# Local attention scores over all 128 rows on zero-spread keys, zero-padded values, agents' rows by broadcast load, and a new step order

## What is computed

```python
x = LN(x + agent_tok * agent_v[:, None, :])          # agent_v: one row of 256 per batch
x = LN(x + cross_attention(x, ctx, masks))           # ctx has 361 rows, one head
x = LN(x + attention over the top 50 tokens, 16 heads)
# local attention: 16 heads of 16 columns, keys within 64 positions
q, k, v = x @ Wq.T + bq, x @ Wk.T + bk, x @ Wv.T + bv
scores = einsum('bhtd,bhtwd->bhtw', q, kb) / sqrt(16);  scores = where(valid, scores, -inf)
x = LN(x + merge_heads(softmax(scores) @ vb) @ Wo.T + bo)
x = LN(x + cross_attention(x, ctx))
x = LN(x + quantize(rms_norm(x)) @ w_int8.T + bias)
```

## Time and profile before

| | |
|---|---|
| runs (3) | 1148.42, 1149.96, 1151.2 us, median 1149.96 us |
| the profiled execution | 1141.62 us, span 1139.5 us |
| granted PE clock, mean over the span | 0.861 of full speed |
| busy: PE, DVE, ACT, POOL | 85%, 62%, 48%, 28% of the span |

### The profile page before, as it was taken

How to read it: one execution, slowest core, us unless ns; L and a number is a source line. 1 busy time by engine, 2 the same in 40 slices (tenths; PEclk the granted TensorE clock), 3 DMA queues, 4 the chain that set the end, 5 groups by cost and what they waited for, 6 DMA issues and landing times.

```text
span 1139.5 us, 19498 instructions
## 1 busy us (share of the span) xinstructions
PE 963.4 (85%) x6958; PEld 706.0 (62%) x6958; DVE 705.2 (62%) x2131; ACT 542.9 (48%) x2440; POOL 315.8 (28%) x460
## 2 busy tenths in 40 slices
PE   6887988989787999886798799899899889998774
PEld 4665776656565766664476586466557666665552
DVE  4226675457787765535777755365848875556664
ACT  3112446667334257654434436556534345675431
POOL 0045211133542220403442320033344330122231
PEclk9857999879898899887889897688679798899676
DMA  7904100002221000010213000002201200000000
GB/s 206 279 22 134 36 2 1 1 21 81 83 89 70 15 1 2 22 54 28 77 40 122 16 1 2 1 22 75 76 28 55 70 15 1 1 2 1 8 8 15
DMA packets 21429, 50.78 MB, mean 45 GB/s; under 512 B 3376, under 2 KB 9236, under 8 KB 21332
## 3 DMA queue, kind: packets, MB, share of 16 engines
q1 hardware_dynamic: 21332, 49.53, 13.3%
HBM read 46.25 MB, written 3.28 MB: 43 GB/s over the span
## 4 chain that ended last, share of the span: by engine, by line
PE 52%; DVE 23%; ACT 17%; issue 3%; POOL 2%; DMA 1%; SPq 1%; DVEq 0%; POOLq 0%
PE psum L419 8%; PE psum L458 8%; ACT work L779 8%; PE psum L424 6%; ACT work L738 5%; PE psum L590 5%; PE psum L444 4%; DVE bn L896 4%; PE psum L604 3%; DVE x L903 2%; PE psum L596 2%; PE psum L610 2%; DVE res L944 1%; DMA ctxT<-in_x 1%; PE psum L414 1%
## 5 line engine op out<-in xcount | busy, mean ns | idle before, releaser
L779 ACT ACTIVATE work<-psum,mx 100x100 f32<-100x100 f32 x512 | 169.9, 381 | 63.3 <-DVE mx L1052 63.1
L779 ACT ACTIVATION_READ_ACCUMULATOR work<-psum,mx 100x1 f32 x512 | 124.6, 245 | 0.0
L1138 POOL TENSOR_SCALAR ve<-mv 100x2 f32<-100x2 f32 x96 | 22.4, 233 | 335.3 <-DVE mv L898 335.1
L458 PE MATMUL psum<-eT,ctx 128*128 128x100 f32 x768 | 102.9, 291 | 3.6 <-DVE eT L932 3.5
L458 PEld LDWEIGHTS psum<-eT,ctx 128*128 128x128 f32 x768 | 99.5, 207 | 6.5 <-DVE eT L932 5.1
L604 PE MATMUL psum<-ident,work 100*100 100x100 f32 x512 | 75.7, 285 | 30.8 <-ACT work L779 30.3
L444 PE MATMUL psum<-ctxT,qT 128*100 128x361 f32 x256 | 91.2, 502 | 5.1 <-ACT qT L669 2.9
L669 ACT ACTIVATE eT<-psum 100x400 f32<-100x400 f32 (+3 forms) x128 | 66.3, 532 | 45.6 <-PE psum L451 21.8
L604 PEld LDWEIGHTS psum<-ident,work 100*100 100x100 f32 x512 | 57.1, 148 | 47.9 <-ACT work L779 43.4
L590 PE MATMUL psum<-kT,qT 32*100 32x200 f32 x512 | 84.5, 410 | 2.7 <-DVE aT L1067 2.4
L1052 DVE TENSOR_REDUCE mx<-psum 100x4 f32<-100x400 f32 x128 | 66.9, 565 | 32.0 <-PE psum L596 31.4
(11 more groups left out here) (234 smaller groups left out, 2184.4 us busy)
## 6 DMA issues: line engine op xcount, KB each, us to landing
ctx<-in_ctx SPq DMA_DIRECT2D x16, 768.0 KB, 6.4
ctxT<-in_ctxT SPq DMA_DIRECT2D x16, 722.0 KB, 4.3
cell<-in_cell SPq DMA_DIRECT2D x16, 282.0 KB
seq<-in_seq SPq DMA_DIRECT2D x16, 282.0 KB
x<-in_x SPq DMA_DIRECT2D x16, 200.0 KB
out<-xplus SPq DMA_DIRECT2D x16, 200.0 KB
work<-in_x SPq DMA_DIRECT2D x4, 400.0 KB
ctx<-in_x SPq DMA_DIRECT2D x2, 400.0 KB
```

Of the source, the lines that this page charges most:

```text
L458: last = e.matmul(bk[b][:, c * S:(c + 1) * S], s.ctx[:, b, j, c * P:(c + 1) * P], s.pT[:, b, j, :], start=j == 0, stop=j == S2C - 1)
L779: last = e.activation(s.e[:, h, :], bk[g][0:S, q * S:(q + 1) * S], ACT.Exp, bias=s.mx[0:S, h:h + 1], accum_out=s.den[0:S, h:h + 1])
```

## The change

- Scores: both key halves leave PSUM with their bias only, into `s.kall`. For each unit POOL writes `s.keys` (128 rows by 8 times 100 columns), the keys multiplied with the constant mask `heads`, so that the columns of head h are zero outside of its 16 rows. Two matmuls over all 128 rows, 400 columns each, give the scores of eight heads, and one mask matmul follows each. The next unit's keys can be written as soon as the scores that read the tile are done.
- Values: `s.v` holds each head's 16 columns padded to 32 with zeros, set once by memset. Two heads then add up in one group of 32 PSUM rows, in 8 matmuls of 32 by 100 in place of 4 of 32 by 200, and nothing has to be picked out. The reciprocals are transposed ahead of them and leave PSUM through ACT meanwhile. DVE line 1064 is gone. One of the two value copies goes to DVE.
- Agents' rows: written once to a DRAM tensor and loaded for each job by a broadcast DMA into the end of `s.eT`; the matmuls of line 474 are gone, and DVE reads the row from SBUF.
- Small tiles of the agents' part share space with others; the memsets to zero of the values are waited for in the pick stage of the first turn and not ahead of it.
- `ORDER` has new strings for all engines.

```diff
-    "local": "xT q k0 k1 v0 v1 " + " ".join(f"hs{i} s{i} tra{i} trb{i} av{i}" for i in range(NB * NC)) + " out0 out1",
+    "local": "xT q k v0 v1 " + " ".join(f"s{i} tra{i} trb{i} R{i} av{i}" for i in range(NB * NC)) + " out0 out1",
...
-                pe, act, dve, pool = s.at("mix")
-                for b in range(NB):
-                    if t:
-                        e.wait_ge(*s.vector["quant"](f"r{b}", t - 1))
-                    n = NB * s.pair(t) + b
-                    e.matmul(bk[b][0:S, 0:D], ident[0:B, n:n + 1].to_broadcast([B, S]), agent_v[:, :],
-                             start=True, stop=True).then_inc(*pe.up(f"agv{b}"))
...
-                    for wave in range(2):
-                        if wave:
-
-                            e.wait_ge(*pe(f"hs{i}", t))
-                        for g in range(2):
-                            r = 32 * (2 * wave + g)
-                            last = e.matmul(bk[g][0:S, wave * T:(wave + 1) * T], s.qT[r:r + 32, c, b * S:(b + 1) * S],
-                                            s.kT[r:r + 32, :, c, b * S:(b + 1) * S], start=wave == 0, stop=False,
-                                            skip_group_check=True)
...
+                    e.wait_ge(*pool(f"bd{i}", t))
+                    for g in range(2):
+                        e.matmul(bk[g][0:S, 0:4 * S], s.qT[:, c, b * S:(b + 1) * S], s.keys[:, 4 * g:4 * g + 4, :],
+                                 start=True, stop=False, skip_group_check=True)
+                        last = e.matmul(edges(bk[g]), band_w[:, :],
+                                        band_x[:, :].rearrange("p (m k) -> p m k", m=2).unsqueeze(1).to_broadcast(
+                                            [NM, 4, 2, NEDGE]), start=False, stop=True, skip_group_check=True)
...
-                    for r in range(ROWS):
-                        e.matmul(bk[0][32 * r:32 * r + 32, 0:T], s.v[0:S, b, c * P + 32 * r:c * P + 32 * r + 32],
-                                 s.eT[0:S, r * T:(r + 1) * T], start=True, stop=True)
-                    e.wait_ge(*pool(f"re{i}", t))
-                    e.transpose(bk[1][:, 0:S], s.rspread[0:S, 0:P], ident[0:S, 0:S]).then_inc(*pe.up(f"av{i}"))
+                    e.wait_ge(*dve(f"eT{i}", t))
+                    e.wait_ge(*pool(f"re{i}", t))
+                    e.transpose(bk[1][:, 0:S], s.rspread, ident[0:S, 0:S]).then_inc(*pe.up(f"R{i}"))
                     e.wait_ge(*act(f"eT{i}", t))
+                    for j in range(2):
+                        for r in range(ROWS):
+                            h = 2 * r + j
+                            last = e.matmul(bk[0][32 * r:32 * r + 32, 0:S], s.v[0:S, b, c * HQ + h, :],
+                                            s.eT[0:S, h * S:(h + 1) * S], start=j == 0, stop=j == 1, skip_group_check=True)
...
-                    e.wait_ge(*act(f"u{i}", t))
-                    e.scalar_tensor_tensor(s.xT[:, 1, 0:S], bk[0][:, S:2 * S], own[:, 1:2], s.xT[:, 0, 0:S], ALU.mult,
-                                           ALU.add).then_inc(*dve.up(f"u{i}"))
...
             for s in streams:
-                last = e.memset(s.v_pick[:, :, :, :], 0.0)
+                e.memset(s.v_pick[:, :, :, :], 0.0)
+                last = e.memset(s.v[:, :, :, :], 0.0)
...
+            def blocks(t, i):
+
+                b, c = divmod(i, NC)
+                if i == 0:
+                    e.wait_ge(*s.vector["local"]("k1", t))
+                else:
+                    e.wait_ge(*s.tensor["local"](f"s{i - 1}", t))
+                e.tensor_tensor(s.keys[:, :, :], s.kall[:, c, b * S:(b + 1) * S].unsqueeze(1).to_broadcast([P, HQ, S]),
+                                heads[:, :].unsqueeze(2).to_broadcast([P, HQ, S]), ALU.mult).then_inc(
+                    *s.gpsimd["local"].up(f"bd{i}"))
...
+            e.wait_ge(*agent_dve("v"))
+            e.dma_start(agent_rows.rearrange("n (b d) -> (n b) d", b=NB), agent_v).then_inc(agent_kept, 16)
+            e.wait_ge(agent_kept, 16)
+            for s in streams:
+                load_agent(e, s, 0)
```

More of the change, by code:

```diff
@@ L97 @@
     "pick": "re ve rstd",
-    "local": "xb " + " ".join(f"re{i}" for i in range(NB * NC)) + " ve rstd",
+    "local": "xb bd0 " + " ".join(f"bd{i + 1} re{i}" for i in range(NB * NC - 1)) + f" re{NB * NC - 1} ve rstd",
     "second": "xb prod qb ve rstd",
@@ L763, in scalar_turns @@
                 yield
[L764 to L768 removed]
+                e.wait_ge(*pe("v0", t))
+                copy(padded(s.v[0:S, 0, :, :]), bk[1][0:S, 0:D].rearrange("p (n j d) -> p n j d", j=2, d=DH)).then_inc(
+                    *act.up("v0"))
                 yield
[L770 to L773 removed]
                 for i in range(NB * NC):
@@ L1257, in sync_first @@
             e.dma_start(wscale[:, :], ins["wscale"].to_broadcast([P, 1])).then_inc(ld_const, 16)
-            for n, tile in (("ident_b", ident_b), ("before", before), ("own", own), ("band_w", band_w), ("band_x", band_x)):
+            for n, tile in (("ident_b", ident_b), ("before", before), ("own", own), ("heads", heads), ("band_w", band_w), ("band_x", band_x)):
                 e.dma_start(tile[:, :], ins[n]).then_inc(ld_const, 16)
```

246 lines of the change are left out of this document (123 added, 123 removed).

## The result

The changed kernel takes 1115.0 us (median of 4 runs, 1113.4 to 1116.4), the kernel before 1150.6 us on the same chip; the ratio is 0.968, 95% interval 0.964 to 0.972. Three more series of runs, on three chips, gave 0.965, 0.967 and 0.969, a mean of 0.967 over all four. Ratios and clock medians leave out executions more than 1.5% longer than the fastest of their kernel. The forecast was 1139 us, so the sign was right, the time lies inside the range, and the gain is 35.6 us where 11 were forecast. The profiled execution takes 1115.85 us, 25.8 less than that of before, because before's was one of its fastest.

The account below looks back on a forecast made before the run. The middle part was taken as bound by PE, but not PE alone, with waits for ACT's exponentials. Terms -9 - 8 - 5 + 9 + 4 - 3 = -12 us, put on the median 1149.96 and rounded to 1139 us; range 1105 to 1172.

Parts of the forecast that it names:

- The clock: PE's mean clock, 0.861: 0.02 shifts 19 us either way, sign unknown; a lower clock alone turning the sign had 0.04.
- The scores: PE, local stage: a unit goes from 1.55 to 1.70 us, +11 us over 64 units, bounds -8 and +29.
- The values: PE's value matmuls: 0.41 us a unit in place of 0.48, -5 us over 64 units, bounds 0 and -17.
- PE's work in all: PE, middle part: -16.1 (agents' rows) + 11 (scores) - 5 (values) = -10 us, times 0.87: -9 us.
- The agents' rows: PE line 474: 64 instructions, 23.2 us, go; 16.1 us of it from the middle part; replacing loads cost nothing.
- ACT and DVE: Copies moved or removed: ACT loses 21.9 us, times 0.36 is -8; DVE net -13.1, times 0.37 is -5.
- The key products: POOL: 64 products of 1.92 us, 123 us more, busy about 439 us; costs +9 us through contention with DVE and queueing.
- DVE's part: DVE's SBUF operations held up by POOL's products: 13 us on DVE, times 0.37, +5 us.
- the queue's part: POOL's short operations queueing behind a product: 22 us, at 0.37 +8, halved to +4 us.
- The rival: POOL's products each hold back a DVE operation, 23 us in place of 5, full queue 8: 1161 us; chance 0.16.
- The start: First transposes at 83.6 us in place of 79.43, behind POOL's zeroing, masks and rstd: +4 us.
- The sequences: New order at the kernel's end: last stages side by side but fewer streams in the last 120 us: -3, from -8 to +6.

Follow-up runs that it names:

- agents_by_dma: The kernel before with only the agents' rows changed to a DMA load, PE's product removed, old sequences kept: ratio 0.992, 9.5 us less.
- new_order_old_work: Changed kernel's sequences and agents' load with the old local-stage work, two steps moved from ACT to DVE: ratio 0.990 to the kernel before, 1139.7 us.
- new_work_old_order: All of the changed kernel's work under the step sequences of the kernel before: ratio 0.995 to the kernel before, 31 us more than the changed kernel.
- after_again: The changed kernel unaltered, run again on the chip of the runs beside it: ratio 0.965 to the kernel before.
- new_order_padded_values: New sequences, old local work plus padded values; differs from the changed kernel by the scores and missing key product: ratio 0.971 to the kernel before, 1124.0 us.
- new_order_full_scores: Changed kernel with values unpadded as before; scores over 128 rows and POOL's key product stay: ratio 0.971 to the kernel before, 1122.3 us.
- no_key_product: Changed kernel with POOL's key product left out (2 of 100 columns written), scores reading unmasked keys: ratio 0.950 to the kernel before.
- key_product_twice: Changed kernel with each key product done twice over the same tile on POOL: ratio 0.997 to the kernel before, 1152.1 us.
- scores_over_32_rows: Changed kernel with score products contracted over rows 0 to 31 instead of all 128: 1186.8 us, ratio 1.028 to the kernel before.

## Why the prediction was wrong

- **The clock: the step that failed.** The prediction had it as a rival: "Another order shifts these stretches; 0.02 of mean clock is 0.02/0.861 x 963 x 0.87 = 19 us either way. I can't tell its sign". And the sum had zero for it. The order moves the clock little, and once each way: 0.858 to 0.845 (medians of agents_by_dma and new_order_old_work), 0.879 to 0.887 (new_work_old_order and after_again). The rows of the scores move it more: 0.825, 0.861 and 0.887 at 32, 64 and 128 rows of 400 columns. A hint of the sign stood in the trace of before, in the falls behind scores over 32 rows with PE wholly busy, and the change widens these scores to 128. The forecast's own list of signs has this one, a mean clock off 0.861 by more than 0.02: it is 0.885. The size: over the 74 runs of the kernel before that the ratios use, all series together, the clock lies between 0.833 and 0.861 and the time between 1139.7 and 1159.8 us; a straight line through them falls by 6.3 us for each 0.01. From 0.851, their median, to 0.887 it is 23 us, if the line goes on that far; it is a correlation within one kernel, and accounts for 73% of the spread. The split of the two profiles gives C 36 us.
- **The scores: right for a unit.** Forecast 1.70 us a unit at the full clock, measured 1.67, from 499.44 to 501.11 in the changed kernel. In all they were dearer than the +11 forecast: W rises by 13 from new_order_padded_values to the changed kernel and by 23 from new_order_old_work to new_order_full_scores. That the mask would cost half of the old pair's was right, by the weight load beside the score.
- **The values: 0 in place of -5** in busy time (39.5 us, 39.4 in before's line 610). As a part of their own they bring 5 us next to the wide scores and 21 without them (7 to 13 and 16 by the times). The prediction costed DVE 1064 by its busy time alone.
- **PE's work in all: nearly right.** Forecast -17 with the start's 7.1, W fell by 11.
- **The agents' rows: right**, -10 forecast with the start, -9.5 measured.
- **ACT and DVE.** ACT fell by 27 us (21.9 forecast). DVE rose by 12 (6 to 7 by the other three profiles) where the steps should have lowered it by 13, and the product's hold on it is the reason, by no_key_product 19 to 24 us; 5 more come with the agents' rows, now read from SBUF (710.7 us in agents_by_dma).
- **The key products: mis-sized, +20 in place of +9.** A product took 1.54 and not 1.92 us, POOL is at 419 us and not 439, and yet the price is double. DVE's part was forecast at 13 us and measured at 19 to 24; the queue's part was taken at half, and no run measures it by itself. The rival, with 22 us more than forecast, was about as near as the forecast: per us of POOL the product costs 0.20 us of time, and a second one 0.35, where the forecast had 9/123 = 0.07 and the rival 31/123 = 0.25.
- **The start: right**, 83.3 us against 83.6, and by the chain that was given for it. One term was luck: the 75.8 from which the sum sets out is 1.5 more than its 70.05 + 4.2, without a source, and the trace has 75.79.

```profile
75.79 1.71 POOL L1153 TENSOR_TENSOR cell<-cell,seq 100x722 f32<-100x722 f32 x1
...
78.62 0.48 DVE L942 SCALAR_TENSOR_TENSOR res<-eT,tok,x 100x256 f32<-100x256 f32 x1
...
81.99 0.71 POOL L1123 TENSOR_TENSOR rstd<-ve,minus_half 100x2 f32<-100x2 f32 x1
...
83.29 0.90 PE L413 MATMUL psum<-ident,x 100*128 100x100 f32 x4 [10.96 <-DVE x L882]
```

- **The sequences: -3 in place of anything up to -31.** The forecast looked at the end only, which hardly changed: PE idles 29.3 of the last 80 us before and 27.7 of the last 74 after. With the old local work -3 is about right (2.5 us), with the new it is not.

Put together, -12 forecast, -23 for the clock and +11 for the product make -24; the gain is 36 to 40 us in the four series. The 12 to 16 us left over are of the size that the sequences could give. With the clock at the 36 us of the two profiles nothing would be left over. The parts don't add up one by one either (the padded values alone are worth 21 or 5 us, the order 2.5 or 31), and I leave them unsplit: how much of the gain is the clock's and how much the sequences' stays open. Shown by single edits are the rows' effect on clock and time and the price of the product; that the sequences work through the waits for exponentials and reciprocals is read from two profiles and not tried by itself.

## What to carry to other kernels

Price a PE-bound change twice: its work at the full clock, and the share of its busy time that will run at half. A matmul that uses few rows is dear in both: here it kept the next weights from loading beside it, and it went with a lower granted clock for everything around it, so laying operands out with zeros to fill 128 rows can pay although it computes eight times what is needed. And where a hand-made order comes with new work, test the two apart: here neither had a gain clear of the noise without the other.

## What the runs showed of the hardware

- The same 256 score instructions of 400 columns: a granted clock of 0.825, 0.861 and 0.887 (medians) at 32, 64 and 128 rows, and 1187, 1153 and 1109 to 1115 us. The kernel with 64 rows also has half the product on POOL. Keys without the spread zeros do not lower the clock: no_key_product has 0.896, with less work on POOL besides.
- More idle time of PE in all did not lower the clock. Before to after, idle grows from 176 to 198 us and the clock from 0.861 to 0.885; key_product_twice has the most idle time, 224 us, at 0.882, and scores_over_32_rows nearly the least, 173 us, at 0.826. The Trainium skill, page "TensorE: Matmul & The Clock Gate", section "HAM oscillation — how this bites in real kernels", puts a throttled clock down to gaps in PE's work. With scores over 128 rows the traces agree, as none of 416 falls comes behind 4 us that were more than 95% busy; with 32 and 64 rows 18 of 211 do, which gaps do not explain.
- Weights over 70 rows load beside a matmul over 128 rows, and not beside one over 64 (0.79 and 1.10 us from score to score).
- An SBUF product of 800 elements a row with both inputs broadcast takes POOL 1.54 us, 1.9 ns an element, less than the 2.4 of its plain sum of 722 (1738 ns); 400 elements take 0.86 us. The same product takes DVE 0.99 to 1.04 us.
